# Attention's tail in an order of its own, and latents and logits of the next batch in the second experts

## The chip, the cores and the metric

The kernel runs on one core of a Trainium2 chip. A core has TensorE (PE, matmuls), VectorE (DVE), ScalarE (ACT), GpSimd (POOL) and SyncE (SP, which issues most DMAs); they run side by side and wait for each other on semaphores. The metric is the device time of one execution in microseconds (us); lower is better.

## The reference

Two layers on 8 sequences of 1024 tokens of 128 features. Each layer is attention plus experts, both from the same normalized input, added to the stream:

```python
x = L0_attn_h_t                                  # (8, 1024, 128)
xn = _layernorm(x)
x = x + _L0_attn_ref(xn, ...) + _L0_ffn_ref(xn, ...)
xn = _layernorm(x)
x = x + _L1_attn_ref(xn, ...) + _L1_ffn_ref(xn, ...)
```

The first layer's attention has 8 heads; keys and values are made from a latent of 32 numbers a token, `c_kv = xn @ W_DKV + b_DKV`. Its experts (8, two chosen for each token) are routed by logits `xn @ router_w.T`. The second layer's attention is a linear "flow" attention of 16 heads (sigmoids of queries and keys, their sums over all tokens, conserved flows), and its experts (8, four chosen for each token) are computed for all tokens. Everything is float32.

## The kernel before, in words

A loop over the 8 sequences (batches). For each, the kernel goes through attention's first run of 32 tiles (heads 0 to 3; a tile is one head's 128 queries against 1024 keys), the chosen experts in 23 blocks, attention's second run of 32 tiles (heads 4 to 7), attention's tail, and the second experts with the flow attention beside them. Each engine's program writes the order of its work out by hand; engines meet only at semaphores.

**Attention** runs in steps `w`. In step `w` TensorE makes the scores of tile `w` (L1701), transposes the probabilities of tile `w - 2` (L1723) and does one quarter of the values of an earlier group of four tiles (`values(g, i)`, L1738; with the last quarter the scales, L1756, matmuls that spread the reciprocal sums of the softmax). VectorE takes the maximum (L1189) and copies the second half of the turned probabilities (L1199); ScalarE takes the exponential (L811) and copies the first half (L795). For some tiles, `both_on_act`, ScalarE copies both halves (L793, L795). ScalarE copies the scales (L801), and VectorE multiplies values and scales to `o_latent` (L1182). Values and scales of all groups are in PSUM bank 7, so a group's values wait for the scaling of the group before.

**The tail** is part of the same steps. The last tile is transposed in step `2 * QUAD_STEPS + TAIL_STEPS + 1`; from there on TensorE does, in this order: the first output (tokens' tiles 0 to 3, L1771), group 14's last quarter and scales, the transposes of the first norm (L1463) for the next batch, group 15's first quarter, the second output (tiles 4 to 6), group 15's other quarters and scales, latents of tiles 0 to 2 (L1493), the third output (tile 7), the other latents, the logits of the first router (L1502), the transposes of the second norm (L1463), the logits of the second router (L1502). After each output VectorE adds it to the stream (L1236), takes statistics (L926, L931) and a variance (L933), GpSimd raises it to the power of minus one half (L652), and VectorE normalizes (L938). ScalarE copies the turned tokens (L726) and makes the high part `x_high` (L783), VectorE the low part `x_low` (L1172). `route_four` on VectorE (L1140 to L1155) makes the gates.

**The second experts** are 32 units. `gate_up(u)` (L1529, six matmuls) and `down(u)` (L1536) are TensorE's; ScalarE and VectorE limit, ScalarE takes a SiLU, VectorE and GpSimd multiply. Units 0 to 3 stand among the eight QKV tiles (L1550) and the transposes of the gates (L1509). `flow_step(u)` does the flow attention's part in unit `u`: the first sums in unit 4 (L1825), the second sums in unit 12 (L1832, PSUM bank 7). The next batch's keys, which overwrite the first half of its turned tokens, are made in unit 15. `take_latents` on VectorE copies logits (L974) and adds the bias to the latents (L977).

The lines that set the order on TensorE before, in the tail:

```python
                for w in range(PERIOD, 2 * PERIOD):
                    attention_step(w)
                latents(b, 6, range(3, NT))
                router(b, 0, 6, NT * DC)
                transpose_norm(b, 1, 4)
                router(b, 1, 4, 0)
```

## Time and profile before

| | |
|---|---|
| median of 3 runs | 2567.86 us (2567.42 to 2567.93) |
| the profiled execution, its own time | 2568.75 us |
| its span | 2567.0 us |
| TensorE busy | 2326.1 us, 91% |
| VectorE busy | 1987.1 us, 77% |
| ScalarE busy | 1664.6 us, 65% |
| GpSimd busy | 716.1 us, 28% |

The span is the time from the first to the last profiled instruction; 1.75 us of the execution lie around it. Busy shares are means over stages with different bounds, and a busy TensorE is not one at its peak. One batch takes about 314 us; the rows below are of the second one where they say nothing else.

### The profile page before, as it was taken

How to read it: one execution, taken by the hardware profiler on the slowest of the kernel's cores; microseconds unless marked ns; L12 is line 12 of the kernel's file. 1: busy time of each engine (PE TensorE's matmuls, PEld its weight loads, DVE VectorE, ACT ScalarE, POOL GpSimd, SP SyncE). 2: the span in 40 equal slices, each digit the busy share in tenths (PEclk: the TensorE clock that was granted, in tenths of full speed). 3: DMA queues.
4: the chain of work that ended last, by engine and by line, in shares of the span. 5: the costliest groups of instructions: out<-in, count | busy, mean ns of one | idle time of the engine just before them, and what ended most of it. 6: DMA issues, size and time to landing. Idle time of an engine off the chain costs nothing.

```text
span 2567.0 us, 65193 instructions
## 1 busy us (share of the span) xinstructions
PE 2326.1 (91%) x25647; PEld 1674.6 (65%) x25647; DVE 1987.1 (77%) x3451; ACT 1664.6 (65%) x3050; POOL 716.1 (28%) x605
## 2 busy tenths in 40 slices
PE   6989989899898998989989899898998989988998
PEld 3667656675666765667657676566765666656675
DVE  6868877788777787787876878868778697786876
ACT  3956558665586656775567755768457684585845
POOL 2220442205322052221522215212252022520234
PEclk9999999999999999999999999999999999999999
DMA  7110221103111031111211112111121102211022
GB/s 256 43 39 5 95 64 43 42 2 112 47 43 42 22 101 39 47 38 43 83 35 51 34 47 88 32 49 30 63 76 33 47 26 75 68 35 49 19 76 65
DMA packets 99126, 141.37 MB, mean 55 GB/s; under 512 B 11523, under 2 KB 60620, under 8 KB 98316
## 3 DMA queue, kind: packets, MB, share of 16 engines
q1 hardware_dynamic: 90636, 120.41, 14.9%
q0 software_dynamic: 8192, 16.79, 2.3%
q8 instruction: 211, 3.46, 0.6%
q14 instruction: 87, 0.71, 0.1%
HBM read 101.84 MB, written 31.13 MB: 52 GB/s over the span
## 4 chain that ended last, share of the span: by engine, by line
PE 63%; DVE 18%; issue 10%; ACT 8%; DMA 0%; SPq 0%; DVEq 0%; POOL 0%; ACTq 0%; POOLq 0%
PE ps L1529 10%; PE ps L1701 7%; PE ps L1738 7%; DVE neg_max L1189 6%; PE ps L1723 6%; PE ps L1536 6%; PE ps L1611 5%; ACT probs L811 3%; PE ps L1633 3%; PE ps L1486 2%; DVE probsT L1199 2%; DVE ffn L1329 2%; PE ps L1550 2%; PE ps L1502 2%; DVE key_low L967 2%
## 5 line engine op out<-in xcount | busy, mean ns | idle before, releaser
L1189 DVE TENSOR_REDUCE neg_max<-ps 128x1 f32<-128x1024 f32 x512 | 621.6, 1215 | 45.1 <-PE ps L1701 39.2
L811 ACT ACTIVATE probs<-ps,neg_max 128x1024 f32<-128x1024 f32 x512 | 574.0, 1121 | 88.1 <-DVE neg_max L1189 80.5
L1529 PE MATMUL ps<-shared,w_split 128*128 128x512 f32 x1536 | 465.5, 439 | 18.6 <-ACT ffn L862 11.7
L1723 PEld LDWEIGHTS ps<-ident,probs 64*128 64x128 f32 x8192 | 333.5, 144 | 159.4 <-issue 125.1
L696 POOL TENSOR_TENSOR probs<-ffn,shared 128x512 f32<-128x512 f32 x208 | 287.6, 1383 | 421.0 <-DVE ffn L1329 171.8
L1723 PE MATMUL ps<-ident,probs 64*128 64x64 f32 x8192 | 362.9, 230 | 33.8 <-issue 26.8
L1529 PEld LDWEIGHTS ps<-shared,w_split 128*128 128x128 f32 x1536 | 285.4, 191 | 165.4 <-issue 62.9
L1701 PE MATMUL ps<-shared,query_a 64*128 64x512 f32 x1024 | 269.4, 522 | 96.5 <-ACT probs L811 73.1
L862 ACT ACTIVATE ffn<-ps,room_of_gate 128x512 f32<-128x512 f32 x256 | 175.0, 684 | 265.4 <-PE ps L1529 265.4
L1738 PE MATMUL ps<-probsT,latent 128*32 128x128 f32 x8192 | 329.2, 280 | 12.8 <-DVE o_latent L1182 10.4
L795 ACT COPY probsT<-ps 128x512 f32<-128x512 f32 x512 | 300.9, 588 | 15.5 <-PE ps L1723 15.3
L652 POOL TENSOR_TENSOR rstd<-var_eps,minus_half 128x8 f32<-128x8 f32 (+2 forms) x25 | 33.0, 1319 | 773.3 <-DVE var_eps L933 773.3
L1199 DVE COPY probsT<-ps 128x512 f32<-128x512 f32 x352 | 239.4, 680 | 10.6 <-PE ps L1723 9.8
L1701 PEld LDWEIGHTS ps<-shared,query_a 64*128 64x128 f32 x1024 | 101.7, 195 | 201.0 <-ACT probs L811 154.0
L1738 PEld LDWEIGHTS ps<-probsT,latent 128*32 128x32 f32 x8192 | 195.6, 109 | 54.3 <-issue 23.9
L1701 PE MATMUL ps<-key_low,query_b 64*128 64x512 f32 x1024 | 215.3, 416 | 0.0
L1536 PE MATMUL ps<-probs,w_down 128*128 128x512 f32 x416 | 210.7, 593 | 1.0 <-POOL probs L696 1.0
L1611 PE MATMUL ps<-w_res,shared 128*128 x552 | 183.1, 440 | 17.6 <-DVE shared L1260 7.3
L875 ACT ACTIVATE ffn<-ffn,silu_bias 128x512 f32<-128x512 f32 x256 | 185.0, 722 | 7.7
L1316 DVE TENSOR_SCALAR ffn<-ps,b_up 128x512 f32<-128x512 f32 x176 | 131.5, 747 | 53.4 <-PE ps L1529 51.0
L1329 DVE SCALAR_TENSOR_TENSOR ffn<-ffn 128x512 f32<-128x512 f32 x176 | 159.4, 906 | 16.3 <-issue 16.1
L1280 DVE TENSOR_TENSOR ffn<-ffn,ps 128x256 f32<-128x256 f32 x184 | 76.5, 419 | 111.1 <-ACT ffn L837 99.4
(230 smaller groups left out, 3544.2 us busy)
## 6 DMA issues: line engine op xcount, KB each, us to landing
w_split<-w_parts SPq DMA_DIRECT2D x132, 256.0 KB, 2.6
shared<-gate_rows SPq DMA_DIRECT2D x64, 512.0 KB, 4.3
y_rows<-probs SPq DMA_DIRECT2D x40, 256.0 KB, 2.2
x_in<-in_x SPq DMA_DIRECT2D x9, 512.0 KB, 4.1
out<-x_mid SPq DMA_DIRECT2D x8, 512.0 KB, 3.2
ffn<-in_gate_up SPq DMA_DIRECT2D x1, 2048.0 KB, 8.8
probsT<-in_gate_up SPq DMA_DIRECT2D x1, 2048.0 KB, 13.5
w_down<-in_down SPq DMA_DIRECT2D x2, 1024.0 KB
```

Of the source, the lines that this page charges most:

```text
L696: nc.gpsimd.tensor_tensor(ffn_h[u % 5], ffn_gu[:, u % 3, :], gate_bc[:, e % GATE_SLOTS, c * BANK:(c + 1) * BANK], ALU.mult).then_inc(h_rea ...
L795: nc.scalar.copy(half_of(t, 0), half_turned(t, 0)).then_inc(low_copied.sem, 1)
L811: nc.scalar.activation(probs[:, t % 3, :], banks(2 * (t % 2)), ACT.Exp, bias=neg_max[:, t % 4:t % 4 + 1], accum_out=row_sum[:, g % 2, t % ...
L1189: nc.vector.tensor_reduce(neg_max[:, t % 4:t % 4 + 1], banks(2 * (t % 2)), X, ALU.max, negate=True).then_inc(max_ready.sem, 1)
L1199: nc.vector.tensor_copy(half_of(t, 1), half_turned(t, 1)).then_inc(high_copied.sem, 1)
L1329: nc.vector.scalar_tensor_tensor(ffn_gu[:, u % 3, :], ffn_u[u % 3], 1.0 - LIMIT, ffn_s[:, u % 3, :], ALU.max, ALU.mult).then_inc(gu_done.s ...
L1529: mm = nc.tensor.matmul(ps[:, bank, :], w_split[:, f % CHUNK_SLOTS, h, k * P:(k + 1) * P], tokens[:, half], start=(part == 0), stop=(part ...
L1536: nc.tensor.matmul(ps[:, 4 + c, :], w_down[1][:, f, :], ffn_h[u % 5], start=False, stop=(f == E * FH - 1)).then_inc(down_done.sem, 1)
L1611: mm = nc.tensor.matmul(ps[:, j % 2, :], xs_parts[x][:, at], w_res_flat[:, bass.ds(first[j] * 4 + h * 2 * F, 2 * F)], start=(part == 0), s ...
L1701: mm = nc.tensor.matmul(ps[:, 2 * (t % 2) + c, :], q[rows, n * P:(n + 1) * P], k[rows, :], start=(part == 0), stop=(part == 1))
L1723: mm = nc.tensor.transpose(ps[:, turn_bank(t, c), k * HQ:(k + 1) * HQ], probs[rows, t % 3, k * P:(k + 1) * P], ident[rows, rows])
L1738: nc.tensor.matmul(ps[DC * j:DC * (j + 1), 7, 0:P], latent[:, k, :], probsT[:, (g % 2) * QUAD + j, k * P:(k + 1) * P], start=(k == 0), sto ...
```

## The change

Four edits:

- **The tail gets its own lines.** `attention_step` ends with the last tile's transposes (`LAST_STEP`). After it TensorE does the first and second output, all four quarters of group 15's values in bank 6 (`LAST_BANK`; they no longer wait for group 14's scaling), the first norm's transposes, the third output, the second norm's transposes and the second router. VectorE's and ScalarE's parts follow in a matching order; all seven normalizations come after the third output's variance.
- **Latents and logits are one series.** The weights of the latents and of the first router lie side by side (`w_first`, 40 columns), so that one matmul for each tile of tokens gives both. It moves out of the tail to unit 9 of the second experts (`NEXT_LATENTS`) and into bank 7; `take_latents` on VectorE follows in unit 10. TensorE's second sums, which use bank 7, wait for `latent_ready`. In the prologue, too, it is one series.
- **Other tiles are copied whole by ScalarE**: the even ones of the first run instead of the odd, and every eighth from the fourth of the second run instead of from the eighth.
- Waits that guarded bank 6 ahead of the first QKV tile go; the semaphore of the logits counts one a batch.

```diff
 SCALED_LAG = 7
-OUTPUT_STEPS = (PERIOD + QUAD_STEPS + 1, PERIOD + QUAD_STEPS + 3, PERIOD + QUAD_STEPS + 7)
+LAST_STEP = PERIOD + QUAD_STEPS + T_LAG
+LAST_BANK = 6
 OUTPUT_TILES = (range(0, 4), range(4, NT - 1), range(NT - 1, NT))
-EARLY_APPLY = range(0, 3)
-LATE_APPLY = range(3, NT - 1)
 PLACES_STEP = QUERY_LEAD + QUAD - 1 + SCALED_LAG
...
 NORM_APPLY = 17
-NEXT_STEP = PERIOD + QUAD_STEPS + 2
-NEXT_TOKENS_STEP = PERIOD + QUAD_STEPS + 6
+NEXT_LATENTS = 9
 NEXT_KEYS = 15
...
     run, i = divmod(t, NT * QUAD)
-    return i % 2 == 1 if run == 0 else i % 8 == 7
+    return i % 2 == 0 if run == 0 else i % 8 == 3
...
         b_k = sb("b_k", [P, 1])
-        w_dkv = sb("w_dkv", [P, DC])
+        w_first = sb("w_first", [P, DC + E])
+        w_dkv = w_first[:, 0:DC]
         b_dkv = sb("b_dkv", [P, DC])
...
         w_down_flat = w_down[0][:, :, :].rearrange("p f d -> p (f d)")
-        w_router = [sb(f"w_router{l}", [P, E]) for l in range(2)]
+        w_router = [w_first[:, DC:DC + E], sb("w_router1", [P, E])[:, :]]
         b_router = sb("b_router", [P, E])
...
+                def scale_copy(g, bank):
+                    nc.scalar.copy(scale_sb[:, g % 2, :], ps[:, bank, P:2 * P]).then_inc(scale_ready.sem, 1)
+
                 def attention_step(w):
...
                         act.wait_ge(u_ready.sem, u_ready.at(b, g + 1))
-                        nc.scalar.copy(scale_sb[:, g % 2, :], ps[:, 7, P:2 * P]).then_inc(scale_ready.sem, 1)
+                        scale_copy(g, 7)
                     t = tile_of(w)
...
                         router_exp(b, ROUTER_EXP_STEPS.index(w))
-                    if w == NEXT_STEP:
-                        copy_xT(b, 0, 0, 2)
...
                         head_round(b, LATE_HEADS[j], 7, LATE_HEADS[j] - QUAD + 1)
-                for w in range(PERIOD, 2 * PERIOD):
+                for w in range(PERIOD, LAST_STEP):
                     if w == PERIOD + QUERY_LEAD:
...
+                act.wait_ge(u_scaled.sem, u_scaled.at(b, GROUPS - 2))
+                act.wait_ge(u_ready.sem, u_ready.at(b, GROUPS))
+                scale_copy(GROUPS - 1, LAST_BANK)
+                copy_xT(b, 0, 0, 2)
                 copy_xT(b, 1, 2, 4)
...
-                dve.wait_ge(logits_mm.sem, logits_mm.at(b, 1))
-                nc.vector.tensor_copy(logits_first[:, :, :].rearrange("p n e -> p (n e)"),
-                                      ps[:, bank, NT * DC:NT * (DC + E)]).then_inc(logits_taken.sem, 1)
                 dve.wait_ge(latent_mm.sem, latent_mm.at(b, 1))
-                nc.vector.tensor_tensor(latent[:, :, :], ps[:, bank, 0:NT * DC].rearrange("p (n c) -> p n c", c=DC),
+                both = ps[:, bank, 0:NT * (DC + E)].rearrange("p (n c) -> p n c", c=DC + E)
+                nc.vector.tensor_copy(logits_first[:, :, :], both[:, :, DC:DC + E]).then_inc(logits_taken.sem, 1)
+                nc.vector.tensor_tensor(latent[:, :, :], both[:, :, 0:DC],
                                         b_dkv[:, :].unsqueeze(1).to_broadcast([P, NT, DC]), ALU.add
...
+                def scaled(g, bank):
+                    nc.vector.tensor_tensor(o_latent[:, g // NT, g % NT, :], ps[:, bank, 0:P],
+                                            scale_sb[:, g % 2, :], ALU.mult).then_inc(u_scaled.sem, 1)
+
+                def output_added(c):
+                    tiles = OUTPUT_TILES[c]
+                    first, end = tiles[0], tiles[-1] + 1
+                    if c == 0:
+                        dve.wait_ge(combined.sem, combined.at(b, 2 * NT))
+                    dve.wait_ge(o_ready.sem, o_ready.at(b, c + 1))
+                    nc.vector.tensor_tensor(x_mid[:, first:end, :], x_mid[:, first:end, :],
+                                            banks(0)[:, first * P:end * P].rearrange("p (n d) -> p n d", d=D), ALU.add
+                                            ).then_inc(o_added.sem, 1)
+                    dve.wait_ge(o_added.sem, o_added.at(b, c + 1))
+                    return norm_stats(x_mid, tiles)
+
                 def attention_step(w):
...
                         nc.vector.reciprocal(inv_sum[:, g % 2, :], row_sum[:, g % 2, :]).then_inc(inv_ready.sem, 1)
-                    if w - 1 in OUTPUT_STEPS:
-                        c = OUTPUT_STEPS.index(w - 1)
-                        if c == 0:
-                            dve.wait_ge(combined.sem, combined.at(b, 2 * NT))
-                        dve.wait_ge(o_ready.sem, o_ready.at(b, c + 1))
-                        tiles = OUTPUT_TILES[c]
-                        first, end = tiles[0], tiles[-1] + 1
-                        nc.vector.tensor_tensor(x_mid[:, first:end, :], x_mid[:, first:end, :],
-                                                banks(0)[:, first * P:end * P].rearrange("p (n d) -> p n d", d=D), ALU.add
-                                                ).then_inc(o_added.sem, 1)
-                        dve.wait_ge(o_added.sem, o_added.at(b, c + 1))
-                        last = norm_stats(x_mid, tiles)
-                        if c >= 1:
-                            link(last, aggregates_next=True)
-                        if c == 1:
-                            norm_variance(0, NT - 1)
-                        if c == 2:
-                            norm_variance(NT - 1, NT)
-                            norm_apply(1, x_mid, LATE_APPLY)
-                    if w == 2 * PERIOD - 1:
-
-                        dve.wait_ge(rstd_ready.sem, rstd_ready.at(b, 2))
-                        norm_apply(1, x_mid, EARLY_APPLY)
...
                         head_rest(LATE_HEADS[j], 7, LATE_HEADS[j] - QUAD + 1)
-                for w in range(PERIOD, 2 * PERIOD + 1):
+                for w in range(PERIOD, LAST_STEP):
                     attention_step(w)
+                dve.wait_ge(scale_ready.sem, scale_ready.at(b, GROUPS - 1))
+                scaled(GROUPS - 2, 7)
+                output_added(0)
+                link(output_added(1), aggregates_next=True)
+                norm_variance(0, NT - 1)
+                dve.wait_ge(scale_ready.sem, scale_ready.at(b, GROUPS))
+                scaled(GROUPS - 1, LAST_BANK)
+                link(output_added(2), aggregates_next=True)
+                norm_variance(NT - 1, NT)
+                dve.wait_ge(rstd_ready.sem, rstd_ready.at(b, 2))
+                norm_apply(1, x_mid, range(0, NT - 1))
                 dve.wait_ge(rstd_ready.sem, rstd_ready.at(b, 3))
...
-                take_latents(b, 6)
                 split_low()
...
                                                 ALU.mult).then_inc(weighted_q.sem, 1)
+                    if u == NEXT_LATENTS + 1:
+                        take_latents(b, 7)
                     if u == FLOW_CONSERVED[0]:
...
                 for n in tiles:
-                    mm = nc.tensor.matmul(ps[:, bank, n * DC:(n + 1) * DC], xT[0][:, n * P:(n + 1) * P],
-                                          w_dkv[:, :], start=True, stop=True)
+                    mm = nc.tensor.matmul(ps[:, bank, n * (DC + E):(n + 1) * (DC + E)], xT[0][:, n * P:(n + 1) * P],
+                                          w_first[:, :], start=True, stop=True)
                 if tiles[-1] == NT - 1:
...
-            def router(b, l, bank, column):
+            def router(b, bank):
                 for n in range(NT):
-                    if l == 1 and n % 4 == 0:
+                    if n % 4 == 0:
                         pe.wait_ge(xT_ready.sem, xT_ready.at(b, 2 + n // 4 + 1))
-                    mm = nc.tensor.matmul(ps[:, bank, column + n * E:column + (n + 1) * E],
-                                          xT[l][:, n * P:(n + 1) * P], w_router[l][:, :], start=True, stop=True)
+                    mm = nc.tensor.matmul(ps[:, bank, n * E:(n + 1) * E], xT[1][:, n * P:(n + 1) * P], w_router[1],
+                                          start=True, stop=True)
                 mm.then_inc(logits_mm.sem, 1)
...
-                pe.wait_ge(logits_taken.sem, logits_taken.at(b, 1))
-                pe.wait_ge(latent_ready.sem, latent_ready.at(b, 1))
                 qkv_tile(0)
...
             latents(None, 5, range(NT))
-            router(None, 0, 5, NT * DC)
             pe.wait_ge(kq_ready.sem, HALVES)
...
-                def values(g, i):
+                def values(g, i, bank=7):
...
-                            pe.wait_ge(u_scaled.sem, u_scaled.at(b, g))
+                            pe.wait_ge(u_scaled.sem, u_scaled.at(b, g if bank == 7 else g - 1))
                     for k in range(2 * i, 2 * i + 2):
                         for j in range(QUAD):
-                            nc.tensor.matmul(ps[DC * j:DC * (j + 1), 7, 0:P], latent[:, k, :],
+                            nc.tensor.matmul(ps[DC * j:DC * (j + 1), bank, 0:P], latent[:, k, :],
                                              probsT[:, (g % 2) * QUAD + j, k * P:(k + 1) * P],
...
                         for j in range(QUAD):
-                            mm = nc.tensor.matmul(ps[DC * j:DC * (j + 1), 7, P:2 * P],
+                            mm = nc.tensor.matmul(ps[DC * j:DC * (j + 1), bank, P:2 * P],
                                                   inv_sum[:, g % 2, j:j + 1].to_broadcast([P, DC]), ident[:, :],
...
-                    if w == NEXT_STEP:
-                        transpose_norm(b, 0, 2)
-                    if w == NEXT_TOKENS_STEP:
-                        latents(b, 6, range(0, 3))
                     t = tile_of(w)
...
                         transpose_probs(t)
-                    if w in OUTPUT_STEPS:
-                        output(OUTPUT_STEPS.index(w))
                     for i in range(NT // 2):
...
                 chosen_experts(b, attention_tail)
-                for w in range(PERIOD, 2 * PERIOD):
+                for w in range(PERIOD, LAST_STEP):
                     attention_step(w)
-
-                latents(b, 6, range(3, NT))
-                router(b, 0, 6, NT * DC)
+                output(0)
+                output(1)
+                for i in range(NT // 2):
+                    values(GROUPS - 1, i, LAST_BANK)
+                transpose_norm(b, 0, 2)
+                output(2)
                 transpose_norm(b, 1, 4)
-                router(b, 1, 4, 0)
+                router(b, 4)
...
                         mm.then_inc(sums_mm.sem, 1)
+                    if u == NEXT_LATENTS:
+                        latents(b, 7, range(NT))
                     if u == FLOW_SUMS2:
+                        pe.wait_ge(latent_ready.sem, latent_ready.at(b, 1))
                         pe.wait_ge(weighted_q.sem, weighted_q.at(b, 1))
```

Left out of the diff: the declaration of the semaphore `logits_mm` (one a batch instead of two), the loads' names for `w_dkv` and `w_router`, the wait in `route_four` that follows from it, and the inner lines that became `scaled(g, 7)`.

## Rows read from the trace of the kernel before

**Rows 1.** The page's part 4: share of the chain that ended last.

```profile
PE 63%; DVE 18%; issue 10%; ACT 8%; DMA 0%; SPq 0%; DVEq 0%; POOL 0%; ACTq 0%; POOLq 0%
```

**Rows 2.** The chain in the tail: start us, us, engine, tile, line, count.

```profile
551.39 1.98 PE ps L1771 x16
553.37 0.57 PE ps L1738 x16
553.95 0.22 PE ps L1756 x8
554.17 1.02 PE ps L1463 x8
...
555.76 1.53 PE ps L1771 x12
557.30 1.45 PE ps L1738 x48
...
561.48 2.25 PE ps L1502 x16
...
565.52 3.41 PE ps L1502 x16
568.93 2.76 PE ps L1550 x4
571.69 3.38 PE ps L1529 x12
575.07 0.87 PE ps L1509 x8
575.94 1.40 PE ps L1529 x6
```

**Rows 3.** Timeline of VectorE in the tail: start us, us, instruction.

```profile
557.34 0.56 DVE L1236 TENSOR_TENSOR x_mid<-x_mid,ps 128x384 f32<-128x384 f32 x1 [0.96 <-PE ps L1771]
...
561.84 0.28 DVE L1236 TENSOR_TENSOR x_mid<-x_mid,ps 128x128 f32<-128x128 f32 x1
...
562.77 1.36 DVE L938 TENSOR_SCALAR probs<-x_mid,mean_var,rstd 128x128 f32<-128x128 f32 x5
564.05 0.22 DVE L974 COPY logits_first<-ps 128x64 f32<-128x64 f32 x1
564.18 0.41 DVE L977 TENSOR_TENSOR latent<-ps,b_dkv 128x256 f32<-128x256 f32 x1
567.26 1.23 DVE L1172 TENSOR_TENSOR shared<-probsT,shared 128x1024 fp32r<-128x1024 f32 x1 [2.66 <-ACT shared L783]
568.97 0.23 DVE L1140 TENSOR_TENSOR r_d<-ps,b_router 128x64 f32<-128x64 f32 x1 [0.49 <-PE ps L1502]
...
573.87 0.22 DVE L1155 TENSOR_TENSOR gate_w<-r_e,top_c 128x64 f32<-128x64 f32 x1
```

**Rows 4.** Timeline of ScalarE in the tail.

```profile
565.56 0.58 ACT L726 COPY probsT<-ps 128x512 f32<-128x512 f32 x1 [0.27 <-PE ps L1463]
566.18 1.05 ACT L783 CAST shared<-probsT 128x1024 fp32r<-128x1024 f32 x1
```

**Rows 5.** Timeline of GpSimd in the tail.

```profile
559.51 1.52 POOL L652 TENSOR_TENSOR rstd<-var_eps,minus_half 128x7 f32<-128x7 f32 x1 [50.17 <-DVE var_eps L933]
```

**Rows 6.** Stretches: length, busy time of each engine, granted clock, DMA.

```profile
562.70:572.70 10.00, 10.00 (x36) 8.35 (x37) 6.68 (x17) 2.47 (x4) 0.73 (x1) 0.50 0.00 0
...
603.00:611.60 8.60, 7.50 (x25) 4.26 (x24) 8.53 (x8) 4.53 (x7) 5.73 (x5) 1.00 0.37 122
...
876.70:886.70 10.00, 10.00 (x39) 8.56 (x39) 6.30 (x19) 2.47 (x4) 0.72 (x1) 0.50 0.00 0
```

**Rows 7.** Timeline of VectorE in unit 10 of the second experts.

```profile
612.30 1.09 DVE L1329 SCALAR_TENSOR_TENSOR ffn<-ffn 128x512 f32<-128x512 f32 x1
```

**Rows 8.** The chain in unit 12 of the second experts.

```profile
611.77 3.72 PE ps L1832 x16
```

**Rows 9.** The chain in the prologue.

```profile
25.37 3.37 PE ps L1502 x16
```

More of the change, by code:

```diff
@@ L442, in two_layer_kernel @@
         w_loaded = [signal(f"w_loaded{i}", CHUNKS // CHUNK_SLOTS * 16) for i in range(CHUNK_SLOTS)]
-        logits_mm = signal("logits_mm", 2, start=1)
+        logits_mm = signal("logits_mm", 1)
         shift_ready = signal("shift_ready", 3)
@@ L488, in two_layer_kernel @@
             (uq_T, "UQ_T"), (uk_T, "UK_T"), (q_rope, "Q_rope"), (dq_T, "DQ_T"), (b_k[:, :], "b_K"),
-            (w_dkv[:, :], "W_DKV"), (w_router[0][:, :], "router0"),
+            (w_dkv, "W_DKV"), (w_router[0], "router0"),
         ]
@@ L493, in two_layer_kernel @@
             (w_qkv[:, :], "W_QKV"), (w_proj[:, :], "W_PROJ"), (w_down[1][:, :, :], "down1"),
-            (w_router[1][:, :], "router1"), (b_gate[:, :], "b_gate"), (b_up[:, :], "b_up"), (b_down[:, :], "b_down"),
+            (w_router[1], "router1"), (b_gate[:, :], "b_gate"), (b_up[:, :], "b_up"), (b_down[:, :], "b_down"),
         ]
@@ L1137, in route_four @@
                 def route_four():
-                    dve.wait_ge(logits_mm.sem, logits_mm.at(b, 2))
+                    dve.wait_ge(logits_mm.sem, logits_mm.at(b, 1))
                     link(nc.vector.tensor_tensor(
@@ L1181, in attention_step @@
                             next(place)
-                        nc.vector.tensor_tensor(o_latent[:, g // NT, g % NT, :], ps[:, 7, 0:P],
-                                                scale_sb[:, g % 2, :], ALU.mult).then_inc(u_scaled.sem, 1)
+                        scaled(g, 7)
                     t = tile_of(w)
```

## Prediction

> **What bounds the kernel now.** I read the chain that ended last first: TensorE holds most of it, VectorE a good part [rows 1]. A gain has to shorten TensorE's path, or a stretch in which TensorE waits. The change touches the prologue, attention's tail and units 9 to 12 of the second experts, so I read the same chain in the second batch's tail next [rows 2]: from the end of the last transposes (551.39) to the transposes of the gates (575.07) it stays on TensorE, 23.68 us without a wait that counts. The reader should see two kinds of work in it: matmuls that the experts need (outputs, second router, QKV, gate and up), and work that they don't need (the first norm's transposes, the latents between the rows shown, the first router). Then the timelines of VectorE, ScalarE and GpSimd in the same stretch [rows 3 to 5], for how soon the needed work could come if the other went away. Last the stretches by themselves [rows 6]: TensorE's granted clock is 0.50, the lower of its two levels (1.2 GHz), from 562.7 to 572.7, and again at the same place of the next batch; and from 603.0 to 611.6, in units 9 to 12, VectorE is busy for 8.53 of 8.60 us and TensorE for 7.50: there VectorE is the bound, and TensorE has slack.
>
> **The tail, step by step.** I lay the new order out from 551.39, with durations of the chain [rows 2]. Group 14's last quarter of values and its scales now come first: 0.57 + 0.22, to 552.18. The first two outputs: 1.98 + 1.53, to 555.69; the scaled latents that the second needs follow the scales by two short instructions of ScalarE and VectorE and are there in time. VectorE ends the first output's statistics about 555.8, so it adds the second about 555.9 instead of 557.34. From there to the start of GpSimd's power it was 557.34 to 559.51, 2.17 us [rows 3, 5]; the power now starts at 558.1 and ends, 1.52 us long, at 559.6. Meanwhile TensorE does group 15's values in the other bank: 0.57 + 1.45, and 0.22 of scales, to 557.93; the first norm's transposes, 1.02, to 558.95; the last output, a quarter of the first one's 1.98, to 559.5 [rows 2]. VectorE comes from its addition to the normalization in 0.93, as 561.84 to 562.77 [rows 3]: 560.5. Five normalizations took 1.36, so eight take 2.2: 562.7. The last transposes follow in 0.3, ScalarE's copy in 0.6, its cast in 1.05 [rows 4]: the second half of the turned tokens is there at 563.7 instead of 566.14, the high part at 564.8, and VectorE's low part, 1.23 [rows 3], at 566.0.
>
> Which comes last then? VectorE's routing took from 568.97 to 574.01, 5.04 us [rows 3], so the gates are ready at 571.1. TensorE has half of the second router left at 563.7: sixteen matmuls took 3.41 at the low clock, so eight take 1.7, to 565.4; two QKV tiles 2.76 and the first two units' gate and up 3.38 [rows 2], both taken as they stand: 571.6. So TensorE still ends last, and the gates' transposes start 575.07 - 571.6 = **3.5 us sooner**. Bounds: at most 3.9 (VectorE's 571.1 and its signal); and at the low clock throughout, twelve matmuls at twice the 0.23 of the six in 1.40 [rows 2] take 5.6 instead of 3.38, to 573.8, a gain of 1.3. I take 3.5, by the row of the stretch itself, in which the clock rose some 1.1 us into the same twelve matmuls.
>
> What leaves this stretch is more than it gains: the first router's sixteen matmuls, 2.25 [rows 2], are gone for good (latents and logits share each load of 128 tokens), and the latents move. The rest turns into waiting for the normalization: between 559.5 and 563.7 TensorE has only transposes and half a router to do.
>
> **Which tiles ScalarE copies whole.** They stay sixteen in the first run and four in the second. In the first run the scales' copy no longer falls into a step with two other copies, so that ScalarE's burst is shorter, but it may then wait for the scales themselves. I cost it at nothing, since ScalarE's work is the same and the queue of copies and exponentials covers the order; without that cover it is one copy of 0.58 [rows 4] a run, either way. That the last tile's second half is now VectorE's was used above.
>
> **Units 9 and 12.** TensorE gets sixteen matmuls of 40 columns in unit 9. The trace shows none of this width; between 1.7 (half of the 3.41 at the low clock) and 2.25 (the 8 columns at full clock) I take 2.0 us. They run from about 602.9 to 604.9, and unit 10's gate and up end about 606.4, before VectorE comes to them near 608, so they are hidden in TensorE's slack. Without that cover they cost 2.0. But TensorE's second sums, in unit 12, now wait first for the latents on VectorE, and these stand in VectorE's queue behind unit 10's product. The sums began at 611.77 [rows 8]; the product ran from 612.30 for 1.09 us [rows 7]; the two instructions that take logits and latents, 0.22 + 0.41 less their overlap [rows 3], end at 613.9. The sums start **2.2 us later**. Queued behind them on TensorE is unit 13; and VectorE, which waits for the sums themselves, passes the delay on to the flows. So nothing takes the 2.2 back. Bounds: 0, if VectorE came to the product that much sooner, and 2.8, if the taking doesn't overlap and a part of TensorE's 2.0 is not hidden. I take 2.2, by the nearest rows.
>
> **Prologue.** The first router's sixteen matmuls stand in the chain there with 3.37 us, at the low clock [rows 9]. They go: 3.4 us once; bounds 0 (another preparation is late next) and 3.4.
>
> **Sum.** A batch: 2.2 - 3.5 = -1.3 us; eight of them -10.4; prologue -3.4; together -13.8. The profiled execution took 2568.75 us (2567.0 of it the span), 0.9 above the median of the runs, 2567.86; less 13.8 that median gives 2554.1.
>
> **The clock, and a rule.** The low stretch begins during the first router and ends some us after QKV and gate matmuls have begun [rows 2, 6]. By that row dense matmuls that begin 3.5 us sooner raise the clock about as much sooner, and my sum stands. The Trainium skill (TensorE: Matmul & The Clock Gate, Part 1: The HAM clock gate) says that the low clock is the default and that activity releases it; read against this change, the new wait before the second router keeps it low as surely as the routers did, and no gain beyond the order of the work is to be had.
>
> **Rivals.**
> - *The wait in unit 12 doesn't come*: VectorE gets ahead of TensorE by then. A batch gains 3.5: 2567.9 - 28 - 3.4 = 2536.5. For it: 2.2 us is a small lead. Against: VectorE has no idle time to gain it in [rows 6]. 0.10.
> - *The low clock lasts*: it reaches the end of unit 2's gate and up. Twelve matmuls at 5.6 leave a gain of 1.3, unit 2's six at 2.8 instead of 1.40 take 1.4 of it, a batch loses 2.3: 2567.9 + 18.4 - 3.4 = 2582.9, slower. It decides where the twelve take 5.1 us (a gain of 1.8, and a total of zero). For: the low stretch is 10 us long now. Against: it ended once dense matmuls ran. 0.15.
> - *The clock takes the gain back elsewhere*: the low stretches stand 314.0 us apart in successive batches [rows 6]; a batch that is a little shorter may meet them at other places, as at the start of attention. If all of the 1.3 goes: 2564.5, within 0.2%. 0.17.
> - *As forecast*, with a net gain of 0.5 to 2.2 us a batch: 0.58, with 2547 to 2561 as its own range.
>
> **How the numbers follow.** 0.2% is 5.1 us, about what a measurement can tell from no change. Faster: the forecast, the first rival and a little of the third, less the forecast's weak end: 0.67. Same: most of the third and that end: 0.18. Slower: the second: 0.15. The range 2539 to 2573 leaves out the ends of the first and second rivals.
>
> **What would show it.** From the last transposes' end to the gates' transposes some 20.2 us instead of 23.68, with TensorE idle ahead of the second norm's transposes and a low stretch shorter than 10 us. From the gates' transposes to the second sums some 38.9 us, 36.70 now, ended by VectorE's latents. The forecast is wrong if the clock stays low beyond the first two units, if the second sums aren't delayed, or if attention's two runs grow.

## The result, and the profile after

The changed kernel took 2573.6 us, median of 20 runs (2565.73 to 2581.73), beside 2567.89 us of the kernel before (20 runs, 2565.96 to 2576.26). The ratio is 1.0020, 95% interval 1.0013 to 1.0027: about 0.2% slower, where I had forecast 0.5% faster. The profiled execution of the changed kernel took 2581.73 us, the slowest of its twenty and 8 above their median; its span is 2580.0 us, 13.0 more than before's 2567.0.

I cut both traces at eight places of each batch and summed over the eight batches. The table is the bookkeeping for all that follows (us; each place is the start of the group of matmuls named, except the last transposes' end; "the last experts' end" is the start of the transposes of their result). Further down, "the first runs" are the table's first two rows together where eight are meant, and "the second runs" its third, chosen experts included.

| stretch | before | after | difference |
|---|---|---|---|
| start to the first batch's sorted tokens | 124.18 | 119.92 | -4.3 |
| the other seven first runs, to the sorted tokens | 519.97 | 535.36 | +15.4 |
| sorted tokens to the last transposes' end | 896.87 | 900.95 | +4.1 |
| last transposes to the gates' transposes | 188.16 | 159.87 | -28.3 |
| gates' transposes to the first sums | 103.82 | 103.04 | -0.8 |
| first sums to the second sums | 190.96 | 208.24 | +17.3 |
| second sums to the next batch's keys | 89.51 | 99.53 | +10.0 |
| keys to the last experts' end | 447.84 | 447.40 | -0.4 |

The three terms of my sum are there: -28.3, +17.3 and -4.3 (I had -28, +17.6 and -3.4). So are 29.5 us in places that I had not priced: the first runs, the second runs and the stretch behind the second sums.

**The tail** in the timeline of TensorE after, fourth batch (start us, us, instruction; in brackets the idle time before it and what ended it). This answers to [rows 2]:

```profile
1181.18 0.64 PE L1742 MATMUL ps<-probsT,latent 128*32 128x128 f32 x16
1181.64 0.40 PE L1760 MATMUL ps<-ident,inv_sum 128*32 128x128 f32 x8
1181.97 3.39 PE L1775 MATMUL ps<-w_o,o_latent 128*128 128x128 f32 x28
1185.29 1.95 PE L1742 MATMUL ps<-probsT,latent 128*32 128x128 f32 x64
1187.06 0.40 PE L1760 MATMUL ps<-ident,inv_sum 128*32 128x128 f32 x8
1187.39 1.09 PE L1470 MATMUL ps<-ident,x_norm_first 128*128 128x128 f32 x8
1188.32 0.62 PE L1775 MATMUL ps<-w_o,o_latent 128*128 128x128 f32 x4
1190.31 2.12 PE L1470 MATMUL ps<-ident,probs 128*128 128x128 f32 x8 [1.37 <-DVE probs L942]
1192.27 2.72 PE L1509 MATMUL ps<-w_router,probsT 128*128 128x8 f32 x16
1194.85 2.91 PE L1557 MATMUL ps<-w_qkv,probsT 128*128 128x384 f32 x4
1196.98 4.59 PE L1536 MATMUL ps<-shared,w_split 128*128 128x512 f32 x12
1201.41 1.04 PE L1516 MATMUL ps<-ident,gate_w 128*8 128x128 f32 x8
```

VectorE's timeline there, beside [rows 3]:

```profile
1189.92 2.13 DVE L942 TENSOR_SCALAR probs<-x_mid,mean_var,rstd 128x128 f32<-128x128 f32 x8
1194.17 1.23 DVE L1175 TENSOR_TENSOR shared<-probsT,shared 128x1024 fp32r<-128x1024 f32 x1 [2.12 <-ACT shared L782]
...
1200.20 0.22 DVE L1158 TENSOR_TENSOR gate_w<-r_e,top_c 128x64 f32<-128x64 f32 x1
```

The reader should see the order that the prediction laid out, with the one wait that it named: TensorE stands for 1.37 us ahead of the second norm's transposes. The eight normalizations end 10.80 us after the last transposes' end (1192.05 from 1181.25; 11.3 forecast), the gates are ready 19.17 us after it (1200.42; 19.7 forecast), and the gates' transposes follow at 20.16 (20.2 forecast).

**The clock in the tail** is not the same in every batch. Stretches from the last transposes to the gates' transposes, second to fourth batch after (length, busy time of each engine, granted clock, DMA):

```profile
548.65:567.88 19.23, 17.40 (x176) 13.67 (x177) 13.67 (x48) 5.35 (x10) 2.24 (x2) 0.91 0.01 2
861.87:883.34 21.47, 20.10 (x176) 16.39 (x177) 15.28 (x50) 5.35 (x10) 2.24 (x2) 0.76 0.01 2
1181.25:1201.41 20.16, 18.79 (x177) 15.14 (x178) 14.60 (x49) 5.35 (x10) 2.24 (x2) 0.83 0.01 2
```

The same work takes 19.23, 20.16 or 21.47 us, and the clock column goes with it: the trace's record of the clock has a low stretch of 3.4, 6.8 and 10.2 us in them. Before, it is 10.2 us in all eight batches (23.5 us each). It also ends sooner now: 16.0 to 20.6 us after the last transposes, 18.0 in the mean, where before it ended after 20.9 to 22.2.

**Unit 12**, fourth batch after, TensorE and then VectorE; this answers to [rows 7, 8]:

```profile
1236.72 1.02 PE L1543 MATMUL ps<-probs,w_down 128*128 128x512 f32 x2
1239.98 5.41 PE L1836 MATMUL ps<-probsT,ones 128*128 128x256 f32 x16 [2.23 <-DVE latent L980]
```

```profile
1238.37 1.09 DVE L1335 SCALAR_TENSOR_TENSOR ffn<-ffn 128x512 f32<-128x512 f32 x1
1239.38 0.21 DVE L979 COPY logits_first<-ps 128x64 f32<-128x64 f32 x1
1239.52 0.41 DVE L980 TENSOR_TENSOR latent<-ps,b_dkv 128x256 f32<-128x256 f32 x1
```

The wait is the forecast one: product, logits, latents, then the sums, 2.23 us idle. What I had not forecast is the line after it: the sixteen sums take 5.41 us, where before they take 3.72 [rows 8]. The stretches say why. First the fourth batch right after the wait, then the second batch, where nothing of it happens:

```profile
1240.00:1243.40 3.40, 3.40 (x10) 2.79 (x11) 1.36 (x2) 0.00 (x0) 2.07 (x2) 0.62 0.00 0
606.57:610.00 3.43, 3.43 (x16) 3.04 (x17) 1.37 (x2) 0.00 (x0) 2.09 (x2) 1.00 0.00 0
```

After the wait the clock is at its lower level (1.2 GHz) for about 3.4 us in six of eight batches, and the stretch from the second sums to the keys is then 12.8 to 12.9 us instead of 11.19: the +10.0 of the table.

**A stop with no wait.** In three of the later first runs TensorE stands still in the middle of a series, with no semaphore behind it. The longest, in the timeline of TensorE:

```profile
1693.79 0.39 PE L1760 MATMUL ps<-ident,inv_sum 128*32 128x128 f32 x4
1696.57 0.41 PE L1760 MATMUL ps<-ident,inv_sum 128*32 128x128 f32 x4 [2.39 <-issue]
```

The DMA view of the same 15 us (busy tenths in 40 slices, GB/s, queues): the sorted tokens are being loaded, and in that crowd the instruction queue moves two packets:

```profile
DMA  2300500000495889999999999300000000002000
GB/s 76 98 0 0 175 0 0 0 0 0 60 208 137 186 289 366 355 306 273 284 311 279 279 350 257 82 5 5 11 16 5 0 0 0 0 0 44 0 0 0
...
q8 instruction: 2, 0.03, 1.0%
```

The stops last 0.69, 1.06 and 2.39 us (fourth to sixth batch), 4.1 in all. Before has none.

### The profile page after: what moved, and what is told of

It reads as the page before. It is cut to its first block and busy times, and to the rows that moved or that the text cites. A ratio compares the mean times of both kernels' runs of the same rounds, so it can differ in the third digit from the quotient of the medians.

```text
span 2580.0 us, 64897 instructions
## 1 busy us (share of the span) xinstructions
PE 2314.5 (90%) x25503; PEld 1661.8 (64%) x25503; DVE 1987.1 (77%) x3451; ACT 1664.8 (65%) x3050; POOL 715.9 (28%) x605
## 5 line engine op out<-in xcount | busy, mean ns | idle before, releaser
L1536 PE MATMUL ps<-shared,w_split 128*128 128x512 f32 x1536 | 476.1, 447 | 10.2 <-ACT ffn L866 10.2
L1727 PEld LDWEIGHTS ps<-ident,probs 64*128 64x128 f32 x8192 | 340.6, 145 | 169.1 <-issue 130.0
L1742 PE MATMUL ps<-probsT,latent 128*32 128x128 f32 x8192 | 329.3, 281 | 13.7 <-DVE o_latent L1179 12.8
```

The source lines that it names most:

```text
L1536: mm = nc.tensor.matmul(ps[:, bank, :], w_split[:, f % CHUNK_SLOTS, h, k * P:(k + 1) * P], tokens[:, half], start=(part == 0), stop=(part ...
L1727: mm = nc.tensor.transpose(ps[:, turn_bank(t, c), k * HQ:(k + 1) * HQ], probs[rows, t % 3, k * P:(k + 1) * P], ident[rows, rows])
L1742: nc.tensor.matmul(ps[DC * j:DC * (j + 1), bank, 0:P], latent[:, k, :], probsT[:, (g % 2) * QUAD + j, k * P:(k + 1) * P], start=(k == 0), ...
```

## The experiments

Twelve kernels, in three groups of four; each group shared its runs of the kernel before. Ratios are to those, with 95% intervals. Profiled values come from one execution each, and executions of one kernel differ: the changed kernel's twenty have mean granted clocks of 0.955 (2581.58 us) to 0.965 (2567.79 us). So a few us between two profiles can be the execution's.

**The choice of tiles, undone and alone.** In the changed kernel, and the other way round in the kernel before:

```diff
-    return i % 2 == 0 if run == 0 else i % 8 == 3
+    return i % 2 == 1 if run == 0 else i % 8 == 7
```

> The changed kernel with the tiles that ScalarE copies whole as they were before (odd ones of the first run, every eighth from the eighth of the second). Theory: the choice of tiles costs the first run 0.7 us and the second 0.6 us a batch of its own, so the sum over eight batches falls by 10 us and the ratio to the kernel before by 0.4 of a hundred; the first run's first four-tile group takes 8.8 us again instead of 9.4. Rival: the choice is innocent and attention grows because the low-clock stretches now meet it elsewhere; then the groups stay at 9.4 and the time within 2 us.

> The kernel before with only the new choice of tiles copied whole by ScalarE. Theory: 10 us slower than the kernel before (2578), with the first group of the first run at 9.4 us instead of 8.8 and the last tiles of the second run later by 0.6. Rival (the low clock's place makes attention longer): no change within 2 us.

Undone: 2569.97 us, 0.9998 (0.9986 to 1.0009). Alone: 2578.25 us, 1.0034 (1.0022 to 1.0046). So the choice that I costed at nothing costs 0.34% by itself, some 9 us. In its trace the first runs take 654.74 us (644.15 before) and the second runs 901.41 (896.87), while the tails are 7.9 us shorter. Undoing it in the changed kernel brings those back (641.37 and 897.17) and removes the stops, but the gain is only 0.2%, where I expected 0.4%. In the profiled execution low stretches now lie at the first sums in seven of eight batches: first to second sums is 27.3 to 28.9 us there, 25.82 in most batches of the changed kernel. The record has 227 us of low clock in all, 215 in the changed kernel and 201 before.

Is the choice's cost only low clock, then? The third batch's first run, in the kernel before and in the changed kernel, has the same mean clock and no stop:

```profile
679.17:753.53 74.36, 64.75 (x1170) 46.74 (x1171) 63.10 (x108) 64.80 (x125) 18.03 (x18) 0.93 0.18 51
```

```profile
673.93:749.42 75.49, 65.06 (x1170) 46.83 (x1171) 64.05 (x108) 64.85 (x125) 18.02 (x18) 0.93 0.18 50
```

It is 1.13 us longer. Over all traces here, a first run with 6.8 us of low clock and no stop takes 74.7 to 75.1 us with the new choice (nine of them) and 73.9 to 74.2 us with the old one (nine). So some 0.8 us a batch is the choice's own, at equal clock.

**The latents in bank 6**, which nothing uses between the first sums and the next batch: TensorE's wait for them moves from the second sums to the next use of bank 6.

```diff
-                        latents(b, 7, range(NT))
+                        latents(b, 6, range(NT))
...
-                        pe.wait_ge(latent_ready.sem, latent_ready.at(b, 1))
```

> The changed kernel with the series of latents and logits in PSUM bank 6 instead of 7, still in unit 9; so TensorE's second sums (bank 7) need not wait for VectorE's taking, only the transposes behind them (bank 6) do. Theory: the wait was the cost. From the first sums to the second 23.7 to 24.0 us instead of 25.82, the low clock after it goes, from the second sums to the key projection 11.2 to 11.8 instead of 12.8 in most batches; in all 2.5 to 3 us a batch, 20 to 24 us less than the changed kernel. Rival: TensorE's own sixteen matmuls are the cost; then the first distance stays at 25.8 and nothing is gained.

2554.63 us, 0.9952 (0.9940 to 0.9965), 19.0 us less than the changed kernel (20 to 24 expected). The second sums come 23.69 us after the first again in six of eight batches, and the keys 11.2 after them in all. The sixteen matmuls are still in unit 9, so they are indeed hidden. The wait in unit 12 and the low clock behind it cost 0.7% together, more than the change lost; 24 of the 27 us between the two profiles lie there.

**The latents in the tail's idle time**, between the last output and the second norm's transposes, in bank 7; VectorE takes them after its last normalization.

```diff
                 output(2)
+                latents(b, 7, range(NT))
                 transpose_norm(b, 1, 4)
```

> The changed kernel with the same series put into the tail, between the last output and the second norm's transposes, in bank 7, and the taking on VectorE right behind the normalizations. Theory: TensorE waits there anyway, so the tail from the last transposes to the gates' transposes stays at 19.2 to 20.5 us, the units have 23.7 and 11.2 us again as in the kernel before; 26 us less than the changed kernel. Rival: the series delays the second norm's transposes and keeps the clock low, the tail grows by 2 us to 22.3 and 16 of the 26 us are lost.

2557.97 us, 0.9957 (0.9945 to 0.9970). TensorE's timeline of the third batch:

```profile
865.07 1.98 PE L1499 MATMUL ps<-w_first,xT_first 128*128 128x40 f32 x16 [0.27 <-ACT xT_first L725]
866.88 1.41 PE L1469 MATMUL ps<-ident,probs 128*128 128x128 f32 x8
868.19 1.95 PE L1508 MATMUL ps<-w_router,probsT 128*128 128x8 f32 x16
870.00 1.54 PE L1556 MATMUL ps<-w_qkv,probsT 128*128 128x384 f32 x4
871.35 3.05 PE L1535 MATMUL ps<-shared,w_split 128*128 128x512 f32 x12
876.34 1.04 PE L1515 MATMUL ps<-ident,gate_w 128*8 128x128 f32 x8 [1.94 <-DVE gate_w L1158]
```

The sixteen matmuls of 40 columns take 1.98 us (2.0 was my price), where TensorE had idled. With that gap filled this batch has no low stretch, nor have four others; the second router takes 1.95 instead of 2.72, and TensorE then waits 1.94 us for VectorE's gates. So 19.23 us is VectorE's floor for this tail, and what lies above it in the changed kernel is the low clock's. The whole kernel gained 15.6 us and not the 26 that I expected: in five batches a low stretch now lies at the first sums, and first to second sums is 25.2 to 26.7 us there.

**Both cures with the old tiles.**

> The changed kernel with both undone at once: the series in bank 6, and the old choice of tiles copied whole. Theory (the two costs are separate): the two gains add up; from 2554.6 for the bank alone down by the 9.5 us that the new tiles cost by themselves, to about 2545. Rival (the low clock takes back what a batch gains): 2552 or more, with low-clock stretches between the first sums and the second in most batches, as the old tiles alone had them.

> The changed kernel with the series in the tail's wait and the old choice of tiles. Theory: 2558.0 less 9.5, about 2548, and no stop in the middle of a series of TensorE, since those came only with the new tiles. Rival (low clock elsewhere): above 2554.

2538.97 us, 0.9893 (0.9877 to 0.9910), and 2539.54 us, 0.9886 (0.9870 to 0.9901): both beat both kernels, by 1.1% and more, and both are 6 us or more below what adding the separate gains gave (2545 and 2548). The first one's unit 12 has neither wait nor low clock:

```profile
908.73 1.02 PE L1543 MATMUL ps<-probs,w_down 128*128 128x512 f32 x2
909.85 3.72 PE L1835 MATMUL ps<-probsT,ones 128*128 128x256 f32 x16
```

The choice of tiles is worth 0.6% here (0.9952 against 0.9893), nearly three times what it was in the changed kernel. Its record has 164 us of low clock, bank 6 with the new tiles 204, and the medians of the mean clock over all executions agree with that (0.967 and 0.958). So a cost isn't the same in each company; that the low stretches are why is argued from these sums, not shown.

**The wait filled.** Three matmuls of 384 columns into an idle bank, right before the wait in the changed kernel (extra work, whose result is overwritten):

```diff
                     if u == FLOW_SUMS2:
+                        for n in range(3):
+                            nc.tensor.matmul(ps[:, 6, 0:3 * D], xT[1][:, n * P:(n + 1) * P], w_qkv[:, :],
+                                             start=True, stop=True)
                         pe.wait_ge(latent_ready.sem, latent_ready.at(b, 1))
```

> The changed kernel with three dense matmuls of 384 columns (about 1.9 us; their results are thrown away) in unit 12, where TensorE waits for the latents. Theory: it is the idle engine that brings the low clock behind the wait; the first sums to the second stay at 25.8 us, and from the second sums to the key projection it is 11.2 us in all batches instead of 12.8 in six of eight; the low stretches of 3.4 us near there are gone; 10 us less in the profile. Rival (the low clock comes from the sums themselves or from the place in the batch): 12.8 stays.

2566.63 us, 0.9990 (0.9981 to 1.0000). TensorE, fourth batch:

```profile
1231.00 2.10 PE L1833 MATMUL ps<-w_qkv,probsT 128*128 128x384 f32 x6
1233.41 3.72 PE L1839 MATMUL ps<-probsT,ones 128*128 128x256 f32 x16 [0.31 <-DVE latent L980]
```

The sums start no sooner (208.15 us from first to second sums over eight batches, 208.24 in the changed kernel), but they take 3.72 again, and the keys follow after 11.2 us in all eight batches: 89.59 instead of 99.53. Six more matmul instructions in a batch make the kernel 0.3% faster, though not all of that is theirs: of the 15.9 us between the two profiles 9.9 lie behind the sums, and the first runs are 7.9 shorter and the tails 2.8 longer. The low stretch behind the sums goes in all six batches when TensorE is kept busy, so the idle time ahead of the sums brings it. The Trainium skill (TensorE: Matmul & The Clock Gate, Part 1: The HAM clock gate) has activity release the low clock. I had used that sentence for the wait in the tail and not for the one that I added here; in the trace the low clock follows this wait in six batches of eight.

**The stops moved.** 32 matmuls of 8 columns, whose result nothing uses, ahead of TensorE's first wait:

```diff
+            for _ in range(32):
+                nc.tensor.matmul(ps[0:DC, 4, 0:8], ident[:, 0:DC], ident[:, 0:8], start=True, stop=True)
             pe.wait_ge(prep_sb.sem, PREP_ALL)
```

> The changed kernel with 32 tiny matmuls (128 instructions of TensorE) more in the prologue, where TensorE waits; results thrown away. 
2569.25 us, 1.0006 (0.9996 to 1.0016). The stops are gone from batches four to six; there is one in the first batch and one of 0.40 us in the eighth:

```profile
112.37 0.34 PE L1729 MATMUL ps<-ident,probs 64*128 64x64 f32 x5
114.39 0.58 PE L1729 MATMUL ps<-ident,probs 64*128 64x64 f32 x11 [1.68 <-issue]
```

Counting all of TensorE's instructions in the trace (matmuls, weight loads, semaphore waits, register instructions) up to each stop gives 22465, 29121 and 35777 in the changed kernel, 2497 and 49345 here. Each leaves 193 when divided by 256. So do the stops of every other trace here. TensorE stops at fixed places of its stream of instructions, where one falls into the load of the sorted tokens. Not each such place stops it: in the kernel before, one (15809 instructions in, at 745.0 us) lies in the same load, at 292 GB/s, and TensorE runs on; the changed kernel has two more of these, at 2012.5 and 2327.6 us.

**Each run's choice by itself**, in the kernel before: `i % 2 == 0` for the first run only, then `i % 8 == 3` for the second only.

> The kernel before, with the new choice of the tiles whose two copies ScalarE makes in the first run of 32 only (even tiles instead of odd ones); the second run's choice is the old one. The first two runs with the choice alone gave, over eight batches, 654.74 us from the end of the last transposes to the sorted tokens where the kernel before has 644.15, and 901.41 us for the second run where it has 896.87, and a tail shorter by 7.9. Theory, the copies' place against ScalarE's scale copy costs time in each run by itself: the first run 652 to 655 us (8 to 10.6 us more), the second run 896 to 898, the tail 187 to 189, time 1.003 to 1.004 of the kernel before. Rival, the choice costs nothing by itself and the low clock and the stops made the difference: the first run within 3 us of 644, time 0.999 to 1.001.

> The kernel before, with the new choice in the second run only (tiles 3, 11, 19 and 27 of its 32 instead of 7, 15, 23 and 31). Theory: the second run 900 to 902 us over the eight batches (4 to 5 more than 896.87), the tail shorter, about 180 us instead of 188.16, because VectorE makes the last tile's high copy, the first run within 3 us of 644.15; together 0.9980 to 0.9995 of the kernel before. Rival, the whole 8 us of the choice lie in the second run and its stops: 1.002 to 1.004.

First run: 2573.81 us, 1.0016 (1.0006 to 1.0026); its profiled execution, 2566.57 us, is the fastest of its ten. Second run: 2568.53 us, 1.0006 (0.9993 to 1.0019). The first runs take 653.17 us with the first (9.0 more, two stops of 1.17 and 0.97 us among them), the second runs 899.73 with the second (2.9 more). The tails were a miss, and an instructive one. I had expected the first kernel's at 187 to 189 us and the second's at 180, with VectorE's copy of the last tile as the reason. They are 177.32 and 185.49. The third batch's tail of the first kernel, whose last tile is copied as before:

```profile
864.89:887.07 22.18, 22.18 (x208) 18.84 (x209) 13.87 (x49) 5.84 (x11) 2.24 (x2) 0.85 0.00 1
```

In both kernels a tail with 6.8 us of low clock takes 22.0 to 22.3 us; one with 10.2 takes 23.5 in the second as in the kernel before. So whoever copies the last tile, the length goes with the low clock. Why the first run's choice shortens a low stretch in the tail is open.

ScalarE's timeline in the third batch's first run, in the kernel before and then with the new choice in the first run only:

```profile
737.15 0.58 ACT L793 COPY probsT<-ps 128x512 f32<-128x512 f32 x1
737.63 0.59 ACT L795 COPY probsT<-ps 128x512 f32<-128x512 f32 x1
738.11 0.29 ACT L801 COPY scale_sb<-ps 128x128 f32<-128x128 f32 x1
738.26 1.14 ACT L811 ACTIVATE probs<-ps,neg_max 128x1024 f32<-128x1024 f32 x1
```

```profile
735.96 0.60 ACT L795 COPY probsT<-ps 128x512 f32<-128x512 f32 x1
736.71 0.27 ACT L801 COPY scale_sb<-ps 128x128 f32<-128x128 f32 x1
736.87 1.12 ACT L811 ACTIVATE probs<-ps,neg_max 128x1024 f32<-128x1024 f32 x1
```

With one copy less ahead of it, ScalarE gets to the scales before they are there (0.75 us from one start to the next, 0.48 before), and the exponential of the next tile stands behind that wait.

**One whole tile fewer.** Bank 6, the old choice in the first run, and tiles 7, 15 and 31 in the second.

> The changed kernel with the latents in bank 6, the old choice of tiles in the first run, and in the second run only tiles 7, 15 and 31 of its 32 whole on ScalarE, so that VectorE copies tile 23's high half as well. In the traces a group of four tiles of the second run with such a tile lasts 8.23 us, and one without it 7.88. Theory, ScalarE sets the pace there: 0.35 us a batch less, 2.8 us in all, 0.986 to 0.989 of the kernel before, beside 0.9893 of the same kernel with four tiles. Rival, VectorE, with one more copy of 0.5 to 0.6 us, becomes the bound in that group: 0.3 us a batch more, 0.990 to 0.992.

2540.12 us, 0.9894 (0.9877 to 0.9910), the same as with tile 23. A miss again: the group of tiles 20 to 23 stays at 8.23 us, and the group after it, which took 7.88, takes 8.23 as well. The second runs take 899.06 us in the profile, 896.49 with tile 23, which is the 0.3 us a batch of the rival, VectorE as the bound. A tile that ScalarE copies whole shortens the group behind it by 0.35.

**A control**: the kernel before with the 32 matmuls.

> A control: the kernel before with 32 matmuls of 8 columns ahead of TensorE's first wait in the first batch; nothing else is changed, and they run while TensorE waits for the weights. Rival, the small shift of the order changes the clock's low stretches as well: their sum moves by more than 10 us from 200.8, and the time by more than 0.2%.

2567.45 us, 0.9993 (0.9984 to 1.0003), with no stop in the trace and 200.7 us of low clock: a small shift of the stream alone does nothing measurable.

## Why the prediction was wrong

Two steps failed: the choice of tiles was put at nothing, and the wait in unit 12 was priced at its own length alone.

- **"I cost it at nothing" (the choice of tiles)**: failed. It had been bounded at 0.58 us a run, 9.3 us for sixteen runs, but neither the sum nor a rival took it in. Alone it costs 0.34%, some 9 us. In the profiles it is 9 to 11 us in the first runs, 2 of them stops and some 6 at equal clock (0.8 a batch), and 3 to 4.5 in the second. The cover that I named, ScalarE's queue, does not hold. That ScalarE's wait for the scales is the mechanism is argued from one place of the timeline, not shown.
- **"So nothing takes the 2.2 back"**: true, and too little. The wait also brings 1.7 us of low clock behind it in six batches, 10.0 us. I had weighed the clock for the wait in the tail and not for the one that I added in unit 12. Filling the wait takes that cost away: this one is shown.
- **The stops**, 4.1 us of the profile: in no case of mine. They occur in all seven traces with the new choice in the first run and in none of the seven without it. That they sit at fixed places of the stream is shown; why only some of these places stop TensorE, and why the old choice is spared, isn't.
- **The tail, -3.5 a batch**: right in size (-3.54 in the mean), in part by luck. At equal low stretches the new order saves 2.0 us (10.2 us of it: 23.5 to 21.5; 6.8: 22.2 in the kernels with new tiles to 20.2). The other 1.5 come from a low stretch shorter than 10.2 us in seven of eight batches, and I had written that no gain beyond the order of the work was to be had. That the clock would rise some 3.5 us sooner holds in the mean (3.2). Inside the layout two errors cancel: in the batch shown QKV ends 15.7 us after the last transposes and not 16.8, and the twelve matmuls of gate and up take 4.4 us and not 3.38.
- **Unit 9 and the 2.2 us in unit 12**: right. The matmuls in unit 9 are hidden, the sums start 2.16 us later in the mean.
- **Prologue**: -4.3, forecast -3.4.

What the sum had right shows where both failed steps are undone: without the wait it gives the first rival's 2536.5 us, and the kernel with the latents in bank 6 and the old tiles took 2538.97.

My priced terms come to -15.3 us in the profile (forecast -13.8). On the other side stand 15.4 in the seven later first runs (of which the choice alone gives 9 to 11, stops included; the changed kernel's stops are 2 us longer; some 3 to 4 are unassigned), 4.1 in the second runs and 10.0 behind unit 12. With the small rows that is the +13.0 of the spans. By medians the loss is 5.7. The third rival, the clock taking the gain back elsewhere, was the nearest, though it limited the loss to the gain. What decides where the low stretches fall in a batch stays open.

## What to carry to other kernels

Price a wait on a busy TensorE twice: its own length, and the low clock that may follow it; where independent matmuls can fill it, try it: here even useless ones paid. A reordering of "the same work" in a stage where ScalarE or VectorE sets the pace isn't free until each queue is laid out step by step, and a bound written down for it belongs in the range. Compare a stretch between kernels only at equal clock: the same tail read 19.2 to 21.5 us in one execution.

## What the runs showed of the hardware

- TensorE can stop for 0.4 to 2.7 us with no wait, at places that are multiples of 256 of its instructions apart. All stops here fall into a load that keeps the DMA engines full (some 300 GB/s), but some such places in the load bring no stop. A batch of 6687 or 6720 instructions isn't a multiple of 256, so a stop comes and goes over the batches.
- A wait of 2.2 us on TensorE between other matmuls was followed by 3.4 us of low clock in six batches of eight; with 2.1 us of matmuls in it, in none.
- Executions of one kernel differ in low clock: the changed kernel's twenty have mean granted clocks of 0.955 to 0.965 and times of 2565.7 to 2581.7 us, and the longer ones tend to have the lower clock. A profile is one of them. The profiles of the two best kernels have 164 and 195 us of low clock, but the first is of its kernel's fastest execution (2536.25 us) and the second of its kernel's slowest (2548.11), while the medians are equal within 0.6 us.
